# Attention on one core: where VectorE's copy of the next step's third transposes stands against the jump of its loop

## The chip, the cores and the metric

One Trainium2 chip, of which the kernel uses one core. The time is device microseconds from launch to end. Three runs of the kernel before gave a median of 2756.42 us (2753.38 to 2757.85).

## The reference, cut to what matters

128 graphs of 128 nodes with 512 features each go through attention with 16 heads of 32 (the adjacency added twice as a bias), a residual and a layer norm, then through one of four expert layers picked for each graph, batch norm statistics per expert, and a second residual and layer norm. All in float32.

```python
a = einsum('bhnd,bhmd->bhnm', q, k) * scale + (adj + adj)
p = softmax(a); o = einsum('bhnm,bhmd->bhnd', p, v)
x = layernorm(x + o @ Wo.T)
out = adj @ (x @ expert_w[top1(x)])
x = layernorm(x + relu(batchnorm_of_expert(out)))
```

The change touches the attention; the other stages are the same code in both kernels.

## The kernel before, in words

The kernel has three stages one after the other: `attention_phase` (L45), `expert_phase` (L636) and `norm_phase` (L907). Each engine has its own program, written out by hand, and engines meet only at semaphores.

In the attention a step is one graph. `for_steps` (L142) runs a loop of 15 rounds with 8 steps written out in each (`TAIL = 2 * UNROLL`), and then the last 8 steps written out behind the loop, without one. At the end of each round every engine jumps back to the start of its own loop.

What one step t does, as far as the change goes:

- TensorE transposes the softmax's 16 heads in four groups c = 0 to 3 into four PSUM banks (L292, semaphore `pt_ps`). With part of the values of step t+2 in between (L233), it multiplies the transposed groups with the values (`weighted_values`, L300), also in four groups. Group c waits at L297 until its transposes have been copied to SBUF: ScalarE copies the odd groups (L415, `pt_odd`), VectorE the even ones (L522, `pt_even`). Then come the scores of step t+1 (L244), the rest of the values, three passes of a projection of queries or keys (L225), the output projection (L356), which waits for `o_lo_done`, and three passes of a second projection.
- ScalarE, once the weighted values are there, writes their high part `o_hi` (L418).
- VectorE subtracts it to get the low part `o_lo` (L540), takes the minima of the 16 heads of step t+1 (L466), their largest values and the scales (L475 to L490), adds the residual (L566), takes the layer norm's statistics (L569 to L574), copies group 0 of the next step's transposes (L577, done at L522), evicts a projection (L580, done at L457) and writes the normalised graph `x1` (L584). In the kernel before, the copy of group 2 of the step's transposes stands at the head of the body (L529, done at L522), so in the first of the 8 steps it is the first thing after the jump. In the third step of every four, two casts of 128x1024 (L452) stand between this copy and L540.

So one line, L522, does both copies of a step, and it does group 2 directly behind L584 in the order of the program, with the jump between the two once in eight steps.

`build` (L1219) allocates SBUF in the order of the code. `adj_t` (L1227) is the expert stage's tile of transposed adjacencies; it is four slots of 136 float32 in each partition, 2176 bytes, and the first of all.

Of the kernel before, what the change touches and what calls it, by code (L numbers as in the profile page):

```python
# [18 lines left out]
F32 = mybir.dt.float32  # L19
# [6 lines left out]
P = 128  # L26
# [3 lines left out]
UNROLL = 4  # L30
# [14 lines left out]
def attention_phase(nc, io, W_hi, W_lo, w_stage, expert_w_in, ident, ones, g_x1, adj_t, hand_over, kept, pair,  # L45
# [11 lines left out]
    def columns(half):  # L57
        return slice(0, GN) if half is None else slice(half * HALF_N, (half + 1) * HALF_N)
# [21 lines left out]
    with ExitStack() as ctx:  # L80
# [69 lines left out]
        def exists(step, last, ahead):  # L150
            return not last or step + ahead < B

        def place_of(t, k, last):

            return (units_so_far(t) + k) % 2 if last else k % 2
# [283 lines left out]
        def _(dve):  # L439
# [5 lines left out]
            def rest_of_expert(e):  # L445
                dve.wait_ge(e_hi_done, e + 1)
                nc.vector.tensor_tensor(W_lo[:, e], w_stage[:, e % 2], W_hi[:, e].bitcast(F32),
                                        ALU.subtract).then_inc(e_lo_done, 1)

            def cut_xt(par, half):  # L450
                at = columns(half)
                nc.vector.tensor_copy(xt_hi[:, par, :, at], xt_stage[:, :, at]).then_inc(xt_hi_done, 1)  # L452

            def copy_qk(n, u, half, par):
                c, which, at = u % C, u // C, columns(half)
                dve.wait_ge(qk_ps, n + 1)
                nc.vector.tensor_scalar(qk[par][which][:, c, at], bank[BANK_A][:, at],  # L457
                                        HALF_SCALE if which == Q else 1.0, None, ALU.mult).then_inc(qk_done[1], 1)

            def minima(t, s):  # L460

                dve.wait_ge(adj_in[s], (t - s) * 4 + 16)
                dve.sem_inc(minima_begun, 1)
                for h in range(HEADS):
                    c, r = h // HC, h % HC
                    nc.vector.tensor_tensor_reduce(neg_s[:, h * P:(h + 1) * P],  # L466
                                                   bank[r][:, c * P:(c + 1) * P], adj_nat[:, s],
                                                   -2.0, BIG, ALU.add, ALU.min,
                                                   neg_max[:, h:h + 1]).then_inc(min_done, 1)
# [9 lines left out]
            def inverse(t, c):  # L479

                heads = slice(c * HC, (c + 1) * HC)
                dve.wait_ge(exp_done, HEADS * t + HC * (c + 1))
                nc.vector.reciprocal(inv_sum[:, heads], row_sum[:, heads]).then_inc(inv_done, 1)
# [36 lines left out]
            def copy_pt(t, c):  # L520
                dve.wait_ge(pt_ps, 4 * t + c + 1)
                nc.vector.tensor_copy(probs_t[:, c * D:(c + 1) * D], bank[c][:, :]).then_inc(pt_even, 1)  # L522

            copy_pt(0, 0)
            copy_qk(4 * C + 1, 1, None, 1)

            def body(t, s, i, g, last):
                more = exists(t, last, 1)
                copy_pt(t, 2)  # L529
                if s == 2 and not last:  # L530

                    dve.wait_ge(v_ps, t + 2)
                    dve.sem_inc(xt_turn, 1)
                    dve.wait_ge(xt_in, i * 16 + 32)
                    for half in range(2):
                        cut_xt(g, half)
                if last and t >= B - 2:
                    rest_of_expert(t - (B - 2))
                dve.wait_ge(o_hi_done, t + 1)
                nc.vector.tensor_tensor(o_lo[:, :, :], bank[BANK_O][:, :].rearrange("p (c n) -> p c n", c=C),  # L540
                                        o_hi[:, :, :].bitcast(F32), ALU.subtract).then_inc(o_lo_done, 1)
                if more:

                    dve.wait_ge(s_ps, t + 2)
                    minima(t + 1, (s + 1) % UNROLL)
                    largest(t + 1, 0)
                    inverse(t + 1, 0)
                    scales(t + 1, 0)
                    largest(t + 1, 1)
                    inverse(t + 1, 1)  # L550
                    scales(t + 1, 1)
                    largest(t + 1, 2)
                here = [(unit, k) for k, unit in enumerate(units_of_step(t, s, g, last)) if place_of(t, k, last) == 1]
                for unit, k in here:
                    if k == 0:
                        copy_qk(*unit)
                if more:
                    inverse(t + 1, 2)
                    scales(t + 1, 2)
                    largest(t + 1, 3)  # L560
                    inverse(t + 1, 3)
                    scales(t + 1, 3)

                dve.wait_ge(wo_ps, t + 1)
                dve.wait_ge(x_in[s], i * 16 + 16)
                nc.vector.tensor_tensor(res[:, s % 2], bank[BANK_WO][:, :], x_nat[:, s],  # L566
                                        ALU.add).then_inc(res_done, 1)
                dve.wait_ge(res_done, t + 2)
                nc.vector.bn_stats(stats[:, s % 2], res[:, s % 2]).then_inc(stats_done, 1)  # L569
                dve.wait_ge(stats_done, t + 1)  # L570
                dve.sem_inc(stats_go, 1)
                nc.vector.bn_aggr(mean_var[:, s % 2], stats[:, s % 2]).then_inc(mv_done, 1)
                dve.wait_ge(mv_done, t + 1)
                nc.vector.tensor_scalar(var_eps[:, s % 2:s % 2 + 1], mean_var[:, s % 2, 1:2], EPS, None,  # L574
                                        ALU.add).then_inc(ve_done, 1)
                if more:
                    copy_pt(t + 1, 0)  # L577
                for unit, k in here:
                    if k > 0:
                        copy_qk(*unit)  # L580

                dve.wait_ge(rstd_done, t + 1)
                dve.wait_ge(x1_out[s], i * 16 + 16)
                nc.vector.tensor_scalar(x1[:, s], res[:, s % 2], mean_var[:, s % 2, 0:1],  # L584
                                        rstd[:, s % 2:s % 2 + 1], ALU.subtract,
                                        ALU.mult).then_inc(x1_done, 1)

            for_steps(dve, body)
            rest_of_expert(V)
# [629 lines left out]
def build(nc, io, out_dram, B, D, E):  # L1219
    C = D // P  # L1220
    x1_dram = nc.dram_tensor("x1_scratch", [B, P, D], F32, kind="Internal").ap()
    y_dram = nc.dram_tensor("y_scratch", [B, P, D], F32, kind="Internal").ap()
    with ExitStack() as ctx:
        def sb(name, shape, dt=F32):
            return ctx.enter_context(nc.sbuf_tensor(name, shape, dt))

        adj_t = sb("adj_t", [P, UNROLL, P + 8])  # L1227
        w_stage = sb("w_stage", [P, 2, C, D])
        expert_w_in = [ctx.enter_context(nc.semaphore(f"expert_w_in{e}")) for e in range(E)]
        ident = sb("ident", [P, P])  # L1230
        ones = sb("ones", [P, P])
        expert_row = sb("expert_row", [1, B], U32)

        def sem(name):
            return ctx.enter_context(nc.semaphore(name))

        e_hi_done, e_lo_done = sem("e_hi_done"), sem("e_lo_done")
        g_x1_in = [sem(f"g_x1_in{i}") for i in range(UNROLL)]
        g_adj_in = [sem(f"g_adj_in{i}") for i in range(UNROLL)]
        ones_done = sem("ones_done")  # L1240
        hand_over = e_hi_done, e_lo_done, g_x1_in, g_adj_in, ones_done

        kept = sb("kept", [P, B // KEPT_EVERY, D])
        out_sum, out_sq = sb("out_sum", [P, E, D]), sb("out_sq", [P, E, D])
        with ExitStack() as cut:
            W_hi = cut.enter_context(nc.sbuf_tensor("w_hi", [P, 4, C, D], F32R))
            W_lo = cut.enter_context(nc.sbuf_tensor("w_lo", [P, 4, C, D], F32R))
            g_x1 = cut.enter_context(nc.sbuf_tensor("g_x1", [P, UNROLL, D], F32))
            attention_phase(nc, io, W_hi, W_lo, w_stage, expert_w_in, ident, ones, g_x1, adj_t, hand_over, kept, (out_sum, out_sq),
                            x1_dram, B, D)  # L1250
            expert_phase(nc, io, W_hi, W_lo, w_stage, expert_w_in, ones, expert_row, kept, out_sum, out_sq,
                         g_x1, adj_t, hand_over, x1_dram, y_dram, B, D, E)
        norm_phase(nc, io, ident, ones, expert_row, kept, out_sum, out_sq, x1_dram, y_dram, out_dram, B, D, E)
# [39 lines left out]
```

## Time and profile before

| | |
|---|---|
| median of 3 runs | 2756.42 us (2753.38 to 2757.85) |
| the profiled execution | 2755.41 us |
| its span, first to last instruction | 2753.7 us (1.7 us lie around it) |
| attention, experts, norm | to about 1990 us, to about 2500 us, to the end |
| TensorE, weight loads | busy 96% and 77% of the span |
| VectorE, ScalarE, GpSimd | busy 72%, 54%, 47% |
| granted TensorE clock, mean | 0.993 of full speed |

Busy time is a mean over three stages with different limits; each stage has to be read by itself. In a row of the timeline the first number is the start in us, the second the time from the start of the first to the end of the last instruction merged into it, "xN" how many are merged, and the bracket how long the engine had been idle and what ended that. "issue" means that the engine waited for nothing that the profile shows.

### The profile page before, as it was taken

The page shows a single profiled execution, that of the slowest core. Times are in us where ns is not written, and L with a number is a line of the kernel's source. Part 1 is how long each engine was busy: PE and PEld are TensorE (multiplying, and loading weights), DVE is VectorE, ACT ScalarE, POOL GpSimd, SP SyncE. Part 2 cuts the span into 40 slices and gives each one's busy share as a digit, 9 for nine tenths or more (in the row PEclk, how much of TensorE's full clock was granted, in tenths as well). Part 3 has the DMA queues.
Part 4 walks back from the last instruction along what each step waited for, and adds up shares of the span by engine and source line. Part 5 has one row for each costly group of instructions (what it writes and reads, how often), then busy time and mean ns, then how long its engine had stood idle before and what let it go on. Part 6 is the DMA issues. An engine that isn't in the chain of part 4 may idle for free. (4 is left out here: it accounts for less than half of the span.)

```text
span 2753.7 us, 71041 instructions
## 1 busy us (share of the span) xinstructions
PE 2642.7 (96%) x19802; PEld 2120.2 (77%) x19803; DVE 1994.9 (72%) x8230; ACT 1491.4 (54%) x5270; POOL 1298.3 (47%) x1174
## 2 busy tenths in 40 slices
PE   8999999999999999999999999999899999998776
PEld 7888888888888888888888888887688888884322
DVE  5888787888888888888887878888733333335887
ACT  4656565656556555656565656566544444442444
POOL 2344333334443434344333334443266666666887
PEclk9999999999999999999999999999999999999999
DMA  3111112111111121111112111112244444445999
GB/s 131 56 59 52 61 51 68 60 60 52 60 54 58 56 72 55 57 60 52 60 52 69 58 61 51 61 55 71 79 126 140 131 135 131 139 136 202 398 406 352
DMA packets 166057, 281.21 MB, mean 102 GB/s; under 512 B 18882, under 2 KB 52674, under 8 KB 161218
## 3 DMA queue, kind: packets, MB, share of 16 engines
q1 hardware_dynamic: 147266, 243.36, 26.4%
q10 hardware_dynamic: 18432, 33.56, 3.2%
q8 instruction: 164, 2.69, 0.4%
q14 instruction: 195, 1.60, 0.2%
HBM read 184.57 MB, written 92.27 MB: 101 GB/s over the span
## 5 line engine op out<-in xcount | busy, mean ns | idle before, releaser
L613 POOL TENSOR_TENSOR kept<-kept 128x512 f32<-128x512 f32 x512 | 532.8, 1041 | 1001.2 <-DVE kept L490 975.7
L380 ACT ACTIVATE kept<-kept 128x128 f32<-128x128 f32 x2048 | 793.2, 392 | 137.3 <-DVE kept L466 137.3
L466 DVE CUSTOM_DVE_ANT_0 kept<-att_bank,kept 128x128 f32<-128x128 f32 x2048 | 442.7, 286 | 1.8 <-PE att_bank L244 0.4
L380 ACT ACTIVATION_READ_ACCUMULATOR kept<-kept 128x1 f32 x2048 | 390.3, 191 | 0.0
L415 ACT ACTIVATE kept<-att_bank 128x512 f32<-128x512 f32 x256 | 153.1, 598 | 392.0 <-PE att_bank L292 392.0
L475 DVE TENSOR_REDUCE kept<-kept 128x4 f32<-128x512 f32 x512 | 347.2, 678 | 0.0
L225 PE MATMUL att_bank<-xt_hi,w_hi 128*128 128x512 f32 (+1 forms) x1080 | 280.0, 381 | 13.0 <-DVE w_lo L442 13.0
L225 PE MATMUL att_bank<-xt_lo,w_hi 128*128 128x512 f32 (+1 forms) x1080 | 277.8, 379 | 0.0
L225 PE MATMUL att_bank<-xt_hi,w_lo 128*128 128x512 f32 (+1 forms) x1080 | 277.6, 379 | 0.0
L292 PE MATMUL att_bank<-ident,kept 128*128 128x128 f32 x2048 | 246.0, 273 | 5.0 <-DVE kept L566 4.4
L292 PEld LDWEIGHTS att_bank<-ident,kept 128*128 128x128 f32 x2048 | 230.2, 140 | 25.0 <-DVE kept L566 5.6
L225 PEld LDWEIGHTS att_bank<-xt_hi,w_hi 128*128 128x128 f32 x1080 | 198.5, 189 | 53.4 <-issue 12.6
L540 DVE TENSOR_TENSOR o_lo<-att_bank,o_hi 128x512 fp32r<-128x512 f32 x128 | 88.5, 691 | 208.3 <-ACT o_hi L418 208.3
L225 PEld LDWEIGHTS att_bank<-xt_lo,w_hi 128*128 128x128 f32 x1080 | 198.0, 189 | 39.1
L225 PEld LDWEIGHTS att_bank<-xt_hi,w_lo 128*128 128x128 f32 x1080 | 197.5, 189 | 37.7
L418 ACT ACTIVATE o_hi<-att_bank 128x512 fp32r<-128x512 f32 x128 | 76.6, 599 | 249.3 <-PE att_bank L300 249.3
L522 DVE COPY kept<-att_bank 128x512 f32<-128x512 f32 x256 | 175.8, 687 | 47.3 <-issue 24.5
L606 POOL TENSOR_TENSOR xt_lo<-kept,xt_hi 128x1024 fp32r<-128x1024 f32 x64 | 163.6, 2577 | 98.0 <-DVE xt_hi L452 98.0
L1054 PE MATMUL ps_z<-n_y,ident 128*128 128x512 f32 x256 | 152.1, 678 | 54.9 <-POOL n_y L1174 52.4
L898 POOL TENSOR_TENSOR out_sum<-out_sum,g_out 128x512 f32 x96 | 123.7, 1289 | 134.6 <-ACT g_out L815 134.6
L827 DVE TENSOR_TENSOR products<-ps_y,router_w 128x16 f32<-128x16 f32 x128 | 22.8, 178 | 220.5 <-PE ps_y L741 220.4
L1209 ACT ACTIVATE n_x<-n_x,n_nb,n_rstd 128x512 f32<-128x512 f32 x128 | 104.2, 814 | 131.5 <-POOL n_nb L1191 80.2
(147 smaller groups left out, 5324.3 us busy)
## 6 DMA issues: line engine op xcount, KB each, us to landing
kept<-in_x SPq DMA_DIRECT2D x128, 256.0 KB, 2.6
x_scratch<-kept SPq DMA_DIRECT2D x128, 256.0 KB, 2.0
g_x<-x_scratch SPq DMA_DIRECT2D x128, 256.0 KB, 2.7
n_x<-x_scratch SPq DMA_DIRECT2D x128, 256.0 KB, 7.0
out_x<-n_x ACTq DMA_DIRECT2D x128, 256.0 KB, 5.5
kept<-in_x_t SPq DMA_DIRECT2D x31, 1024.0 KB, 5.2
y_scratch<-g_out SPq DMA_DIRECT2D x96, 256.0 KB, 2.0
n_y<-y_scratch SPq DMA_DIRECT2D x96, 256.0 KB, 6.6
```

Source lines behind the costliest of these rows:

```text
L225: mm = pe.matmul(dst, w[:, which, k, c * P:(c + 1) * P], x[:, par, k, at], start=m == 0, stop=m == len(todo) - 1)
L292: mm = pe.transpose(bank[c][:, r * P:(r + 1) * P], probs[:, h * P:(h + 1) * P], ident[:, :])
L380: nc.scalar.activation(probs[:, h * P:(h + 1) * P], neg_s[:, h * P:(h + 1) * P], ACT.Exp, bias=neg_max[:, h:h + 1], scale=-1.0, accum_out= ...
L415: nc.scalar.activation(probs_t[:, c * D:(c + 1) * D], bank[c][:, :], ACT.Copy).then_inc(pt_odd, 1)
L466: nc.vector.tensor_tensor_reduce(neg_s[:, h * P:(h + 1) * P], bank[r][:, c * P:(c + 1) * P], adj_nat[:, s], -2.0, BIG, ALU.add, ALU.min, n ...
L475: nc.vector.tensor_reduce(abs_max[:, heads], neg_s[:, c * D:(c + 1) * D].rearrange("p (h m) -> p h m", h=HC), AX_X, ALU.max, apply_absolut ...
L522: nc.vector.tensor_copy(probs_t[:, c * D:(c + 1) * D], bank[c][:, :]).then_inc(pt_even, 1)
L606: nc.gpsimd.tensor_tensor(xt_lo[:, par, :, at], xt_stage[:, :, at], xt_hi[:, par, :, at].bitcast(F32), ALU.subtract).then_inc(xt_lo_done, 1)
L613: nc.gpsimd.tensor_tensor(part, part, by, ALU.mult).then_inc(probs_done, 1)
L898: nc.gpsimd.tensor_tensor(acc, acc, src, ALU.add).then_inc(sum_done, 1)
L1054: pe.matmul(dst, ident[:, :], y[:, s], start=True, stop=False)
L1209: nc.scalar.activation(x1[:, s], x1[:, s], ACT.Identity, bias=nb[:, u, k:k + 1], scale=rstd[:, u, k:k + 1]).then_inc(out_done, 1)
```

## The change

VectorE's copy of group 2 for step t+1 is issued at the end of step t's body instead of at the head of step t+1's body; the copy of step 0 is issued once ahead of the loop. And `adj_t` is allocated behind `out_sq`, in the part of SBUF that the norm stage takes over, instead of ahead of everything.

```diff
             copy_pt(0, 0)
             copy_qk(4 * C + 1, 1, None, 1)
+            copy_pt(0, 2)
 
             def body(t, s, i, g, last):
                 more = exists(t, last, 1)
-                copy_pt(t, 2)
                 if s == 2 and not last:
...
                                         rstd[:, s % 2:s % 2 + 1], ALU.subtract,
                                         ALU.mult).then_inc(x1_done, 1)
+                if more:
+                    copy_pt(t + 1, 2)
 
             for_steps(dve, body)
...
-        adj_t = sb("adj_t", [P, UNROLL, P + 8])
         w_stage = sb("w_stage", [P, 2, C, D])
...
         with ExitStack() as cut:
+            adj_t = cut.enter_context(nc.sbuf_tensor("adj_t", [P, UNROLL, P + 8], F32))
             W_hi = cut.enter_context(nc.sbuf_tensor("w_hi", [P, 4, C, D], F32R))
```

## Rows read from the trace of the kernel before

**Rows 1.** Busy time by stretch: undisturbed attention steps; 106 steps with 14 jumps

```profile
core 0: us, PE busy (x) PEld busy (x) DVE busy (x) ACT busy (x) POOL busy (x), PEclk, DMA share, GB/s
161.06:1772.07 1611.01, 1596.52 (x13576) 1315.85 (x13572) 1317.57 (x5671) 957.65 (x3922) 632.74 (x582) 1.00 0.18 59
921.67:1011.83 90.16, 90.16 (x776) 74.56 (x772) 75.08 (x323) 54.20 (x222) 38.52 (x34) 1.00 0.16 53
```

**Rows 2.** Line L522, the copies: count, idle time before them, who waited

```profile
L522 DVE COPY kept<-att_bank x256: 679/690/693, 51.5 to 1973.7; 128x512 f32<-128x512 f32 x128
  issue: 24.5, 14
```

**Rows 3.** TensorE's waits in the attention loop, 60 to 1800 us: total, times, longest

```profile
PE att_bank L300 <- DVE kept L522: 14.1, 14, 1.2
```

**Rows 4.** VectorE's timeline around the jump at 903 us

```profile
901.14 0.69 DVE L522 COPY kept<-att_bank 128x512 f32<-128x512 f32 x1 [0.22 <-PE att_bank L292]
901.75 0.68 DVE L457 TENSOR_SCALAR out_sum<-att_bank 128x512 f32<-128x512 f32 x1
902.35 0.54 DVE L584 TENSOR_SCALAR kept<-kept,mean_var,rstd 128x512 f32<-128x512 f32 x1
904.58 0.69 DVE L522 COPY kept<-att_bank 128x512 f32<-128x512 f32 x1 [1.69 <-issue]
906.66 0.69 DVE L540 TENSOR_TENSOR o_lo<-att_bank,o_hi 128x512 fp32r<-128x512 f32 x1 [1.40 <-ACT o_hi L418]
```

**Rows 5.** VectorE's timeline one step later, without a jump

```profile
918.52 0.54 DVE L584 TENSOR_SCALAR kept<-kept,mean_var,rstd 128x512 f32<-128x512 f32 x1
918.98 0.68 DVE L522 COPY kept<-att_bank 128x512 f32<-128x512 f32 x1
921.67 0.69 DVE L540 TENSOR_TENSOR o_lo<-att_bank,o_hi 128x512 fp32r<-128x512 f32 x1 [2.01 <-ACT o_hi L418]
```

**Rows 6.** TensorE's timeline over the same two steps

```profile
889.59 1.17 PE L244 MATMUL att_bank<-w_stage,g_x 32*128 32x128 f32 x32
...
903.74 0.64 PE L300 MATMUL att_bank<-kept 128*32 128x128 f32 x16
905.33 0.64 PE L300 MATMUL att_bank<-kept 128*32 128x128 f32 x16 [0.94 <-DVE kept L522]
905.90 1.17 PE L244 MATMUL att_bank<-w_stage,g_x 32*128 32x128 f32 x32
...
911.23 1.07 PE L356 MATMUL att_bank<-w_hi,o_hi 128*128 128x512 f32 x4
...
919.89 1.08 PE L300 MATMUL att_bank<-kept 128*32 128x128 f32 x32
```

**Rows 7.** ScalarE's timeline at the jump at 903 us

```profile
902.45 0.60 ACT L415 ACTIVATE kept<-att_bank 128x512 f32<-128x512 f32 x1 [0.28 <-PE att_bank L292]
906.04 0.60 ACT L418 ACTIVATE o_hi<-att_bank 128x512 fp32r<-128x512 f32 x1 [2.98 <-PE att_bank L300]
```

**Rows 8.** VectorE: the copy after the longest and the shortest of 14 jumps; the loop's exit

```profile
418.46 0.69 DVE L522 COPY kept<-att_bank 128x512 f32<-128x512 f32 x1 [1.97 <-issue]
...
1269.13 0.69 DVE L522 COPY kept<-att_bank 128x512 f32<-128x512 f32 x1 [1.47 <-issue]
...
1874.56 0.68 DVE L522 COPY kept<-att_bank 128x512 f32<-128x512 f32 x1
```

**Rows 9.** VectorE by line and shape: one eviction into four tiles

```profile
L457 DVE TENSOR_SCALAR out_sum<-att_bank 128x512 f32<-128x512 f32 x31 | 21.1, 680 | 0.0
L457 DVE TENSOR_SCALAR w_stage<-att_bank 128x512 f32<-128x512 f32 x30 | 20.4, 680 | 0.0
L457 DVE TENSOR_SCALAR g_x<-att_bank 128x512 f32<-128x512 f32 x30 | 20.4, 680 | 0.0
```

**Rows 10.** Busy time by stretch: the norm stage and the expert stage (columns as in rows 1)

```profile
2560.00:2740.00 180.00, 136.56 (x307) 53.99 (x306) 150.89 (x355) 82.94 (x102) 157.22 (x154) 0.96 1.05 404
2010.00:2400.00 390.00, 390.00 (x2107) 332.45 (x2106) 145.10 (x703) 164.00 (x301) 254.46 (x202) 1.00 0.44 135
```

## The prediction, on record before the changed kernel ran

> **What bounds the kernel now.** I read the stages first, by busy time in stretches. Between two jumps of the attention loop TensorE is busy for all of six steps, 90.16 of 90.16 us, so a step there takes 90.16 / 6 = 15.03 us, while VectorE is busy for 75.08 us, 12.5 us in a step [rows 1]. TensorE sets the pace, and VectorE has room. Over 106 steps with 14 jumps in them TensorE is not fully busy: 1596.52 of 1611.01 us [rows 1]. At 15.027 us the 106 steps would take 1592.8 us; they take 18.2 us more, 1.3 us for each jump.
>
> Next, who makes TensorE wait. In this loop there is one large wait: the weighted values wait 14 times, 14.1 us in all, for VectorE's copy of the transposes [rows 3]. Then, why that copy is late. Of the 256 copies 14 stand behind an idle time that no semaphore ended, 24.5 us together, 1.75 us each [rows 2]. The timeline shows which: group 2's copy in the first step of a round. L584 ends at 902.89 us and the copy starts at 904.58 us, after 1.69 us [rows 4]. In the step after, the same two instructions follow each other without a gap [rows 5], and so they do where the loop is left and nothing jumps [rows 8]. 15 rounds have 14 jumps back. What the copy reads was ready long before: ScalarE, which waits for group 3's transposes, later than group 2's, took them at 902.45 us [rows 7]. So the gap is VectorE's jump.
>
> Last, what the gap does to TensorE. Group 0's matmuls start at 903.74 us; the second half (groups 2 and 3), which needs the late copy, starts at 905.33 us, 1.59 us later. Without a jump all 32 follow each other [rows 6]: the row is 1.08 us long against 0.64 us for half of them, so the second half starts 0.44 us after the first. The late copy costs 1.59 - 0.44 = 1.15 us here.
>
> **The change, part by part.** *Removed:* the gap ahead of the copy in 14 steps. The order of VectorE's instructions, the semaphores and their counts stay as they are; the copy issues no DMA and passes no queue; SP's store of x1 waits for L584, which stands ahead of the copy in both kernels. Only the jump moves, behind the copy. With it there, the copy follows L584 as in rows 5, 0.46 us after its start: at about 902.81 us, done at 903.50 us. TensorE wants it at 903.74 + 0.44 = 904.18 us, so 0.68 us of room is left, and the stall goes.
>
> The size of the stall has two ends. The 14.1 us that TensorE's own waits give are the lower one [rows 3]: that view counts idle time after the modelled end of the matmuls before, so it leaves out part of the delay (0.94 us in the row where the starts show 1.15 us). The upper one is the 18.2 us by which the 14 rounds are too long [rows 1], if all of that is VectorE's doing. Not all is: in this round group 0 itself, which waits for no late copy, starts 14.15 us after the scores before it (889.59 to 903.74 us), against 13.99 us a step later (905.90 to 919.89 us) [rows 6]. These 0.16 us come before the stall and stay; 14 x 0.16 = 2.2 us. I take 18.2 - 2.2 = **16.0 us**; 14 x 1.15 = 16.1 us agrees.
>
> *Added:* the jump ahead of L540. What hides it: after the copy, L540 waits for ScalarE's `o_hi`, and that for TensorE, 2.01 us in a step without a jump [rows 5]. The 14 gaps lie between 1.47 and 1.97 us [rows 8], all below 2.01 us, and VectorE may reach the jump a little earlier, since the instruction ahead of it is then 0.69 us long and not 0.54 us [rows 4]. Cost 0. If the cover is short by some tenths, they fall into the next rooms: the output projection wants `o_lo` at 911.23 us, and L540 ends at 907.35 us [rows 4, 6]; the next copy has 0.65 us (it ends at 919.66 us, its matmuls start at 919.89 + 0.44 us [rows 5, 6]). L540 would have to be over 0.65 us late, a jump of over 2.66 us, before TensorE felt it. Behind the copy's own wait only the jump and L540 are queued, and its transposes are in time [rows 7].
>
> What a jump is made of the trace does not say. *The Trainium skill, "Runtime: NRT & Kernel Launch", section "Instruction fetch mechanics", says that a taken branch whose target is not among the two pages held makes the sequencer fetch the page first, a stall. It speaks against getting rid of the jump's price by moving it: by it the same stall stands ahead of L540. With the room of rows 5 it gives the same sum.*
>
> *Ahead of the loop* group 2's copy of step 0 is issued where it was executed anyway: 0. *The last 8 steps* have no jump and keep their order: 0.
>
> *`adj_t`:* the tiles from `w_stage` to `out_sq` and those of the norm stage start 2176 bytes lower in each partition, the others stay. For the engines I take 0: the same eviction takes 680 ns into three tiles at different places [rows 9]. For DMAs no row compares places; the attention's run at a share of 0.18 [rows 1] and the experts' at 0.44 beside a fully busy TensorE [rows 10], so only the norm stage (share 1.05, 404 GB/s [rows 10]) could feel it, either way. I take 0, the nearest thing measured, and put the other end among the rivals.
>
> *Sum:* 16.0 us off the profiled execution's 2755.4 us is 2739.4 us. The median of the runs shown lies 1.0 us above that execution, so like runs would have 2740.4 us; I say **2740 us**.
>
> **The rivals.** *A, the gap is not the jump's and goes with the copy* (something that the first step of a round does ahead of that copy alone). For it: "issue" names no cause. Against it: the gap is missing at the loop's exit, with the same code behind it [rows 8]. TensorE would wait as before: 2755 us. *By the Trainium skill, "Advanced Engine Details and Errata", section "Control Flow Timing", a compare-and-branch takes about 108 ns; with that as the whole jump the change would give 14 x 0.108 = 1.5 us, by an estimate from that page, and the time would be 2754 us. The gaps of 1.47 to 1.97 us do not agree with it as the whole price.* Chance 6%.
>
> *B, the jump is dearer in its new place*, because the loop's start now lies elsewhere in the code and its first instructions come in two loads instead of one. Two gaps are 2 x 1.75 = 3.50 us [rows 2]: L540 would be 3.50 - 2.01 = 1.49 us late, the next copy 1.49 - 0.65 = 0.84 us too late for TensorE. Of 1.15 us for each jump 0.31 us would be won, 14 x 0.31 = 4.3 us: 2751 us. For it: the gaps differ by 0.5 us with nothing in the code to say why. Against it: every one of the 14 is below the cover. 6%.
>
> *C, slower: the lower addresses slow the norm stage's DMAs.* That stage runs at the DMAs' limit for 180 us [rows 10]. To come out slower by over 5.5 us it has to lose 16.0 + 5.5 = 21.5 us, so its transfers would have to take over 12% longer; at 15% it would lose 27 us, and the time would be 2755.4 - 16.0 + 27.0 = 2766 us. For it: no row excludes it. Against it: nothing in the rows makes a place in SBUF matter [rows 9]. 3%.
>
> **How the numbers follow.** The forecast has 85%. Its own range: 14.1 to 18.2 us off 2755.4 us, 2737.2 to 2741.3 us, widened by the 2 us by which the runs differ and the 1.0 us to the median, 2735 to 2744 us. B lies above it at 2751 us, with shares of a second load in between, so I let the range reach to 2746 us: **2735 to 2746 us**. About 0.2%, 5.5 us, is what a measurement here can tell from no change. Faster by more: the forecast and a small part of B, 87%. Within: A and most of B, 10%. Slower: C, 3%.
>
> **What would show it.** Right: in the first step of a round the copy follows L584 without a gap; the idle time ahead of L540 in that step is about 2.0 us, as in other steps; TensorE's wait for L522 in the loop is gone; a round falls from 8 x 15.03 + 1.3 = 121.5 us to about 120.4 us. The steps fail one by one: if "issue" still stands ahead of L522, A; if L540 is ended by "issue" and starts over 0.65 us late, B; if the rounds are shorter and the norm stage longer, C. If rounds shrink by 1.3 us and not 1.15 us, the 0.16 us were VectorE's too, and the gain is the upper end.

## The result, and the profile after

| | before | after |
|---|---|---|
| median (lowest to highest) | 2756.19 us (2753.38 to 2757.85, 4 runs) | 2739.20 us (2738.39 to 2740.26, 4 runs) |
| ratio | | 0.994, 95% interval 0.9922 to 0.9957 |
| the profiled execution, its span | 2755.41 us, 2753.7 us | 2738.80 us, 2737.0 us |

The forecast was 2740 us, in a range of 2735 to 2746 us. The changed kernel is faster by 17.0 us, 0.6%.

The stretch of 106 steps that holds the 14 jumps, by busy time in stretches (columns as in [rows 1]: length, then PE, PEld, DVE, ACT, POOL):

```profile
159.57:1754.84 1595.27, 1594.20 (x13576) 1316.70 (x13572) 1313.26 (x5671) 957.81 (x3922) 632.93 (x582) 1.00 0.18 59
```

It answers to the 1611.01 us of [rows 1]: 15.74 us less, and TensorE is busy in all but 1.1 us of it. The line of the copies, and then TensorE's waits in the loop, 60 to 1800 us, both of the changed kernel:

```profile
L522 DVE COPY kept<-att_bank x256: 679/684/692, 50.0 to 1956.7; 128x512 f32<-128x512 f32 x128
its engine sat idle before it (us, times) until:
  PE att_bank L292: 14.1, 39
```

```profile
PE att_bank L292 <- issue: 0.9, 4, 0.3
```

The 24.5 us by "issue" ahead of L522 [rows 2] are gone, and so are the 14.1 us of TensorE's waits for it [rows 3]. (The 14.1 us in the line above are another wait: 39 short ones of VectorE for TensorE's transposes.) VectorE's timeline around a jump of the changed kernel:

```profile
893.64 0.54 DVE L584 TENSOR_SCALAR kept<-kept,mean_var,rstd 128x512 f32<-128x512 f32 x1
894.09 0.68 DVE L522 COPY kept<-att_bank 128x512 f32<-128x512 f32 x1
896.81 0.69 DVE L540 TENSOR_TENSOR o_lo<-att_bank,o_hi 128x512 fp32r<-128x512 f32 x1 [2.03 <-ACT o_hi L418]
```

This is a step with a jump, and it looks like the step without one in [rows 5]: the copy directly behind L584, then 2.03 us that ScalarE ends. The jump is inside those 2.03 us. One has to know that it is there to find it, since the view gives the whole idle time to what ended it.

The two spans differ by 16.6 us. The 106 steps give 15.74 us of it. 1.49 us were won ahead of them: the same L540 from which the stretch is counted starts at 159.57 us and not at 161.06 us. The rest of the program lost 0.6 us. Nothing ties the 1.49 us to the change: the first experiment found the early and the late start in both places of `adj_t`.

### The profile page after: what moved, and what is told of

Read it like the earlier page. It is cut to its first block and busy times, and to the rows that moved or that the text cites. A ratio compares the mean times of both kernels' runs of the same rounds, so it can differ in the third digit from the quotient of the medians.

```text
span 2737.0 us, 71026 instructions
## 1 busy us (share of the span) xinstructions
PE 2641.8 (97%) x19802; PEld 2120.9 (77%) x19803; DVE 1991.8 (73%) x8230; ACT 1491.7 (55%) x5270; POOL 1301.2 (48%) x1174
## 5 line engine op out<-in xcount | busy, mean ns | idle before, releaser
L292 PE MATMUL att_bank<-ident,kept 128*128 128x128 f32 x2048 | 246.0, 273 | 6.0 <-DVE kept L566 4.7
L292 PEld LDWEIGHTS att_bank<-ident,kept 128*128 128x128 f32 x2048 | 230.1, 140 | 26.6 <-DVE kept L566 5.9
L540 DVE TENSOR_TENSOR o_lo<-att_bank,o_hi 128x512 fp32r<-128x512 f32 x128 | 88.4, 691 | 218.3 <-ACT o_hi L418 218.3
L522 DVE COPY kept<-att_bank 128x512 f32<-128x512 f32 x256 | 175.7, 686 | 22.7 <-PE att_bank L292 14.1
```

The source lines that it names most:

```text
L292: mm = pe.transpose(bank[c][:, r * P:(r + 1) * P], probs[:, h * P:(h + 1) * P], ident[:, :])
```

## The experiments

Ratios are against the kernel before, run on the same chip.

**1. Each half of the change alone.** In `copy_only` the copy is moved and `adj_t` stays the first tile; in `place_only` only `adj_t` is moved.

```diff
 copy_only, against the changed kernel
+        adj_t = sb("adj_t", [P, UNROLL, P + 8])
         w_stage = sb("w_stage", [P, 2, C, D])
...
-            adj_t = cut.enter_context(nc.sbuf_tensor("adj_t", [P, UNROLL, P + 8], F32))
 place_only, against the kernel before: the same two lines the other way round
```

> The copy moved as in the change, adj_t left where it was. Theory (the whole gain is the jump taken off TensorE's path): as the changed kernel, 2739 us, 0.994 of before; in the attention loop TensorE's wait for L522 is gone, the 106 steps take about 1595.3 us as in the changed kernel. Rival (the lower addresses carry part of it, such as the 1.5 us by which the changed kernel's first weights were split earlier): 1.5 us or more above the changed kernel, with the steps equally long.

> Only adj_t moved, the copy at the head of the body as before. Theory: as before, 2756 us, ratio 1.000 within 0.001; 14 gaps of 1.75 us ahead of the copy and 14 us of waits of TensorE for it. Rival (addresses matter for the first loads or for the norm stage's DMAs): at least 1.5 us faster, with the first W_lo written about 1.5 us earlier, or a norm stage longer or shorter by some us.

Measured: `copy_only` 2738.3 us, ratio 0.9938 (0.9924 to 0.9951); `place_only` 2756.82 us, ratio 1.0003 (0.9994 to 1.0012). The 106 steps, first of `copy_only`, then of `place_only`:

```profile
159.44:1754.17 1594.73, 1593.94 (x13576) 1316.69 (x13572) 1313.24 (x5671) 957.62 (x3922) 632.67 (x582) 1.00 0.18 59
```

```profile
160.34:1772.10 1611.76, 1596.50 (x13576) 1315.78 (x13572) 1317.62 (x5670) 958.11 (x3922) 633.77 (x582) 1.00 0.18 59
```

The copy alone gives the whole gain and the tile's place gives none. What of the 1.5 us at the start? The first split of a weight, L442 on VectorE, in the kernel before and in the changed kernel:

```profile
10.58 2.29 DVE L442 TENSOR_TENSOR w_lo<-w_stage,w_hi 128x2048 fp32r<-128x2048 f32 x1 [5.55 <-ACT w_hi L369]
```

```profile
9.03 2.29 DVE L442 TENSOR_TENSOR w_lo<-w_stage,w_hi 128x2048 fp32r<-128x2048 f32 x1 [3.77 <-ACT w_hi L369]
```

`copy_only`, with the tile in its old place, has the early start as well (9.11 us), and two of the kernels below with the tile in its new place have the late one (10.56 us in `delay_16`, 10.52 us in `jump_behind_low`). So the start differs from execution to execution in both layouts, and no row ties it to the tile. What makes it differ stays open.

**2. Is the jump still paid?** `probe_1` puts one tiny copy behind the jump that waits for nothing, so that the time until it starts is the jump's own.

```diff
                 more = exists(t, last, 1)
+                if s == 0 and g == 0 and not last:
+                    nc.vector.tensor_copy(res[:, 0, 0:1], ident[:, 0:1])
```

> The changed kernel with one more instruction on VectorE at the head of every eighth step, a copy of one element per partition that waits for no semaphore, so that the gap ahead of it is the jump's own. Theory: the jump still costs VectorE its time: a gap by issue of 1.4 to 1.9 us ahead of that copy 14 times, nothing ahead of it in the first round; L540 still starts when the high part is there; time as the changed kernel, 2739 us within 2. Rival (behind the copy the jump is no longer dear): gaps under 0.5 us, same time.

Measured: 2740.29 us, one run. The probe's line:

```profile
L531 DVE COPY kept<-ident x15: 144/154/155, 52.7 to 1738.9; 128x1 f32<-128x1 f32 x15
its engine sat idle before it (us, times) until:
  issue: 21.8, 14
```

VectorE still loses 21.8 / 14 = 1.56 us at each jump and the time is that of the changed kernel: the price is paid, and nothing waits for it. It is 0.19 us less than ahead of the copy (1.75 us, [rows 2]).

The rows of VectorE's sequencer (DVEq), in which the loop's own instructions stand, say why the visible part depends on what stands ahead. L144 is the loop; these are VectorE's rows of it in the kernel before, 890 to 910 us (count, shortest/median/longest in ns, start of the first and of the last):

```profile
L144 DVEq COMPARE_BRANCH  x1: 63/63/63, 901.7 to 901.7; - x1
L144 DVEq FUSED_REGOPS  x1: 74/74/74, 904.5 to 904.5; - x1
```

The branch itself takes 63 ns, but the sequencer's next instruction comes 2.8 us after it, and the copy at 904.58 us. VectorE's sequencer got to the branch at 901.7 us, when L584 was queued and not yet begun [rows 4]. The queued work, until 902.89 us, covered 1.2 us; the 1.69 us by "issue" in [rows 4] are what was left. In between, instructions are fetched: a DMA queue of the kind "instruction" in the same kernel, 902.5 to 903.2 us (packets, MB, share of 16 engines):

```profile
q14 instruction: 1, 0.01, 3.9%
```

In the trace of that kernel one such packet of 8 KB starts 0.99 to 1.01 us behind each of the 14 branches, and the next instruction follows 2.77 to 2.97 us behind the branch. The packet itself takes 0.32 to 0.55 us; what fills the rest of the 2.8 us no row shows.

The Trainium skill has two pages on this. "Advanced Engine Details and Errata", section "Control Flow Timing", gives about 108 ns for a compare-and-branch; the branch's own row agrees with that order, the jump as a whole does not. "Runtime: NRT & Kernel Launch", section "Instruction fetch mechanics", says that a branch to a page not held has to wait for its fetch; the trace agrees, with one fetch seen about 1 us behind the branch and 2.8 us in all.

**3. How much cover is there?** The cover is VectorE's wait ahead of L540, behind which the jump hides; the room is how late L540 may come beyond it before TensorE waits. `delay_16` puts a reduction of 2.29 us behind the jump, ahead of L540, in every eighth step.

```diff
+                if s == 0 and g == 0 and not last:
+                    nc.vector.tensor_reduce(res[:, 0, 0:HEADS], ident[:, :].unsqueeze(1).to_broadcast([P, HEADS, P]),
+                                            AX_X, ALU.max)
```

> The changed kernel with a reduction of 16 x 128 elements (about 2.2 us, by the 0.68 us of L475 for 512) at the head of every eighth step on VectorE, behind the jump and ahead of L540. Theory (cover of 2.0 us ahead of L540, then room of 0.65 us at the next copy): jump 1.6 us and 2.2 us are 3.8 us, so L540 is 1.8 us late, the next copy 1.15 us too late for TensorE, which waits for L522 14 or 15 times in the step after the jump: 16 us more than the changed kernel, about 2755 us. Rival (VectorE has 2.5 us free in each step and swallows it): under 3 us more, no wait of TensorE for L522.

Measured: 2753.0 us, 13.8 us more than the changed kernel. TensorE's waits, 60 to 1800 us:

```profile
PE att_bank L292 <- DVE kept L569: 12.0, 14, 0.9
```

The size was nearly right, the place was not. L540 is late by 1.56 + 2.29 - 2.03 = 1.82 us, and 13.8 / 14 = 0.99 us of it reach TensorE, so the room is 0.83 us. But TensorE does not wait for L522. It waits at the head of the next step, at its transposes, for the residual (L569 here, L566 in the kernel before), since L311 asks for `res_done` ahead of everything else. That wait comes before the copies' one and takes up the whole delay.

**4. The jump where nothing hides it.** `jump_behind_low` moves L540 in front of the jump too.

```diff
                 if more:
                     copy_pt(t + 1, 2)
+                    low(t + 1, s == 1, i, g, last)
```

Here `low` holds the casts of the third step and L540, which are taken out of the head of the body, and is called once ahead of the loop.

> The changed kernel with L540 (the low part of the weighted values) and the casts ahead of it moved in front of the jump too, so that the jump stands between L540 and the minima. Theory (the jump keeps its price of about 1.7 us and the wait for ScalarE's high part is what hides it in the changed kernel): here nothing hides it; a gap by issue of about 1.7 us ahead of the first of the minima, 14 times; the next copy is 1.7 - 0.65 = 1.05 us too late for TensorE, 14 x 1.05 = 15 us more than the changed kernel, about 2754 us. Rival (the price belonged to the copy standing first behind the jump, or any later place hides it): no gap, 2739 us.

Measured: 2804.43 us, ratio 1.0177 (1.0162 to 1.0193), 65 us more than the changed kernel and not 15. The order is the only difference, and in the seven steps of eight without a jump it is the same order. VectorE's and TensorE's waits, 60 to 1830 us:

```profile
DVE kept L466 <- issue: 64.3, 14, 5.2
```

```profile
PE att_bank L356 <- ACT kept L386: 37.5, 14, 3.3
PE att_bank L292 <- DVE kept L569: 3.5, 4, 0.9
```

The rival, that any later place hides the jump, falls. But the gap is 4.6 us each and not 1.7 us, and TensorE's waits of 41 us explain less than 65 us. The first has two parts. With L540 in front, VectorE's sequencer stands at L540's wait for ScalarE and gets to the branch only when L540 starts (176.37 us, the branch 176.5 us), so that nothing but L540 itself, 0.69 us, covers the 2.8 us. And the jump itself was longer, in the same rows of L144:

```profile
L144 DVEq COMPARE_BRANCH  x1: 62/62/62, 176.5 to 176.5; - x1
L144 DVEq FUSED_REGOPS  x1: 63/63/63, 181.3 to 181.3; - x1
```

Unrounded, from 176.46 us to 181.33 us, these are 4.9 us. At that time a load of 1 MB was on the DMA engines. SyncE's issues of that load, here and then in the changed kernel, where VectorE's branch is at 171.5 us:

```profile
174.82 0.34 SPq L166 DMA_DIRECT2D kept<-in_x_t  x1
```

```profile
173.37 0.34 SPq L166 DMA_DIRECT2D kept<-in_x_t  x1
```

Here the branch (176.46 us) comes 1.6 us behind the load's issue; in the changed kernel it comes 1.9 us ahead of it. The DMA queues of `jump_behind_low` from 176.4 to 179.0 us, and then from 179.0 to 179.7 us:

```profile
q1 hardware_dynamic: 116, 0.94, 90.4%
```

```profile
q8 instruction: 1, 0.02, 10.5%
q14 instruction: 2, 0.02, 5.6%
```

For 2.6 us after the branch only data moved, at 90% of the engines; then the instructions came. The rest of the 65 us lies behind TensorE's wait at L356. From the first matmul of L356 to the next transposes it took 7.21 us in that step (183.82 to 191.03 us), against 5.44 us in the changed kernel (901.38 to 906.82 us): 1.77 us more. A part of that is TensorE's clock: the granted clock of a stretch of 6.2 us behind the wait is 0.72, so a part of it ran at 1.2 instead of 2.4 GHz:

```profile
183.80:190.00 6.20, 6.17 (x20) 4.93 (x21) 5.68 (x27) 5.46 (x27) 3.38 (x4) 0.72 0.00 0
```

The 14 steps are not all alike. In ten the granted clock behind the wait is down, to 0.62 at the lowest (first row); in four it stays at 1.00 (second row):

```profile
683.00:692.00 9.00, 7.83 (x22) 6.21 (x23) 8.18 (x40) 6.60 (x32) 4.16 (x5) 0.62 0.04 3
1184.00:1192.00 8.00, 5.76 (x24) 4.43 (x24) 7.49 (x43) 7.16 (x34) 3.48 (x4) 1.00 0.00 0
```

Those four are the steps in which TensorE then waits for the residual (3.5 us in all), and they too take 6.63 us from L356 to the transposes, 1.19 us more than in the changed kernel. Over all 14 that stretch takes 7.26 us in the mean, 1.82 us more. So 1.19 us of it would have come at the full clock too, and by this estimate 14 x 0.63 = 9 us of the 65 are the clock's. Counted by starts, L356 itself is 2.87 us late in the mean, and the sum is 14 x (2.87 + 1.82) = 66 us.

**5. Was it the load?** `low_xt_later` is the same kernel with the load issued one step later; `xt_later` is the changed kernel with that edit alone.

```diff
-                if s == 0 and not last:
+                if s == 1 and not last:
                     sp.wait_ge(xt_lo_done, i * 2 + 4)
                     load_xt(i + 2)
```

> The kernel with the jump behind L540 again, with SyncE's load of 1 MB of transposed inputs (L192) issued in the second step of every four instead of the first. Theory (the gaps of 4.6 us there are a jump of 2.8 us whose code waits behind this load, which was on the DMA engines from 1.9 us before the jump to 3 us after it): the gaps ahead of the minima fall to 2.2 to 2.5 us, TensorE waits under 1 us at L356 and keeps its full clock, and 14 x 1.7 us remain over the changed kernel: about 2763 us, 2755 to 2768. Rival (a jump is dearer when VectorE has nothing queued as it reaches it): gaps of 4.6 us, 2804 us as before.

> The control: the changed kernel with the same move of SyncE's load. Theory: VectorE's jump is over before that load starts in the changed kernel, so nothing changes, 2739 us within 2. Rival (the load's place matters by itself): another time by over 2 us.

Measured: `low_xt_later` 2771.63 us, ratio 1.0063 (1.0046 to 1.008); `xt_later` 2739.89 us, ratio 0.9947 (0.993 to 0.9964). Waits of VectorE and of TensorE in `low_xt_later`, 60 to 1830 us:

```profile
DVE kept L466 <- issue: 38.9, 14, 3.0
```

```profile
PE att_bank L292 <- DVE kept L569: 12.5, 14, 0.9
PE att_bank L356 <- ACT kept L386: 12.2, 14, 1.1
```

The gaps fell from 4.6 to 2.78 us, TensorE kept its clock over the loop (1.00, shown at the end), and 33 us of the 65 went away; the control did not move. So the load's place made the jump longer. The rest was mis-sized: 2.2 to 2.5 us of gap and 1.7 us of cost were expected, 2.78 and 2.3 us came (32.4 / 14), which is 9 us more than expected and above the range given. The expectation counted the jump alone; in this kernel it took 3.0 us (175.0 to 178.0 us by L144's rows), and two more instructions of the sequencer (L462, L463) stand between it and the minima. And TensorE waits twice, 12.2 / 14 = 0.87 us for the values at L356 and 12.5 / 14 = 0.89 us for the residual at L292. This view counts only from the modelled end of the matmuls; by their starts L356 is 1.07 us late in the mean and the stretch behind it takes 6.63 us instead of 5.44 us, 2.26 us together.

**6. Fewer jumps.** The loop of one engine alone is written out for 24 steps, so that it has 4 jumps back instead of 14: VectorE's in the kernel before (`dve_24`), TensorE's in the changed kernel (`pe_24`, the same edit with `nc.tensor`).

```diff
-            with eng.Fori(0, LAST // TAIL) as i:
-                for s in range(TAIL):
-                    body(i * TAIL + s, s % UNROLL, i * 2 + s // UNROLL, s // UNROLL, False)
+            n = 3 * TAIL if eng is nc.vector else TAIL
+            with eng.Fori(0, LAST // n) as i:
+                for s in range(n):
+                    body(i * n + s, s % UNROLL, i * (n // UNROLL) + s // UNROLL, s // UNROLL % 2, False)
```

> The kernel before, with VectorE's loop alone written out for 24 steps instead of 8: 5 rounds, 4 jumps back instead of 14; the copy still stands first behind each. Theory (each jump costs TensorE 1.15 us there): 10 x 1.15 = 11.5 us less than before, about 2745 us, 4 gaps ahead of L522 and 4 waits of TensorE. Rival (the gap belongs to the first of eight steps, not to the jump): as before, 14 gaps, 2756 us.

> The changed kernel with TensorE's loop alone written out for 24 steps: 4 jumps back instead of 14. Theory (the 2.4 us that the changed loop still takes over 106 x 15.027 us is TensorE's own jump, up to 0.5 us in some rounds): about 1.7 us less than the changed kernel, 2737.5 us, late first transposes in at most 4 steps. Rival (the late transposes come from what they wait for, GpSimd's scaling or VectorE's residual): nothing won, 2739 us, still 8 or 9 late steps.

Measured: `dve_24` 2743.2 us, ratio 0.9961 (0.9946 to 0.9976); `pe_24` 2738.36 us, ratio 0.9938 (0.9925 to 0.9952). VectorE's waits and the 106 steps in `dve_24` (the copy's line is L523 there), then the 106 steps of `pe_24`:

```profile
DVE kept L523 <- issue: 7.1, 4, 2.2
```

```profile
158.80:1758.40 1599.60, 1594.99 (x13576) 1316.42 (x13572) 1316.35 (x5670) 958.00 (x3922) 633.73 (x582) 1.00 0.18 59
```

```profile
159.47:1752.41 1592.94, 1592.85 (x13576) 1317.09 (x13572) 1313.57 (x5670) 957.84 (x3922) 632.90 (x582) 1.00 0.18 59
```

Ten jumps fewer took ten gaps and 11.4 us of the 106 steps away (1611.01 to 1599.60 us): the gap belongs to the jump, and rival A, which had lost its "issue" ahead of L522 in the changed kernel, falls a second time. In `pe_24` the 106 steps take 1592.94 us, against 1592.83 us for 106 x 15.027, so the 2.4 us that the changed loop still had are put down to TensorE's own jumps. Two things weaken this: four jumps are left in `pe_24`, and yet nearly all of the 2.4 us went; and with all 14 of them the excess was 1.9 us in `copy_only` and 1.0 us in `xt_later` (1593.84 us), so it differs between executions. The whole kernel's time shows it too weakly to count: 2738.36 against 2739.20 us, with intervals that overlap. No version was found that is clearly faster than the changed kernel.

## Why the prediction was right

- *What bounds the kernel:* right. With the wait gone, TensorE is busy for 1594.20 of 1595.27 us.
- *The gap is VectorE's jump:* right. It is gone from L522, it stands in front of whatever is first behind the jump (`probe_1`), and it goes with the number of jumps (`dve_24`).
- *The size, 16.0 us:* the 106 steps became 15.74 us shorter, and 16.28 us shorter in `copy_only`. The upper end, 18.2 us, would have needed that the whole excess was VectorE's. The 2.2 us set aside for what is late before the copy, read off one step, measured 2.4 us here and 1.0 to 1.9 us in other executions; `pe_24` points to TensorE's jump, while the prediction had left them without a cause. The lower end, 14.1 us, was too low for the reason given, the matmuls' modelled ends.
- *Nothing at the jump's new place:* right. The gap there is 1.56 us against a cover of 2.03 us. The slight shortening that was expected, 0.15 us, came as 0.19 us. But the prediction took the visible gap for the jump's price. That the trace does not say what a jump is made of was not so: the rows of L144 and the packet of instructions (experiment 2) are in the trace of the kernel before, and they put the price at 2.8 us, with 1.2 us of it behind queued work. The forecast did not suffer, since work was queued ahead of the jump in its new place too; the expectation of `jump_behind_low` did.
- *The rooms behind the cover:* the size was about right, the place was wrong. The prediction expected 0.65 us at the next copy (its own rows give 919.89 + 0.44 - 919.66 = 0.67 us) and overlooked that TensorE waits for the residual at the head of each step; `delay_16` ran into that wait first, with a room of 0.83 us. Nothing in the forecast hung on it, since the cover sufficed.
- *`adj_t` at nothing:* right (`place_only`, 1.0003). In the changed kernel 180 us of the norm stage (from 2543 us) show 400 GB/s against 404 GB/s in [rows 10]. From TensorE's first matmul of that stage to the end it takes 257.0 us, 1.2 us more than before (255.8 us), but 257.5 us in `copy_only` too, where the tile is in its old place. Rival C, which needed 21.5 us, falls.
- *Rival B, a dearer jump,* did not come true, but a dearer jump was nearer than it said, for another reason: not by where the code lies, but with a load of 1 MB under way, the price rose from 2.8 to 4.9 us in `jump_behind_low`.

A part of the agreement in the whole time is luck. Of the 16.6 us between the two profiled executions 15.74 us are the steps, 1.49 us an early start that differs between executions, and 0.6 us were lost elsewhere; the forecast held neither of the last two, and they partly cancel. What bears out the prediction are the steps and the experiments, not the 0.8 us between 2740 and 2739.2 us.

## What to carry to other kernels

A loop's jump cost VectorE about 3 us here, of which the work queued ahead of it hid a part, so its place matters: put it where the engine will wait for another one anyway, behind the last thing that the bottleneck engine needs from this engine and ahead of an instruction that has a long wait. The sign of a jump is idle time by "issue" in the first step of each round; the gain is not that idle time (24.5 us here) but the amount by which the round with the jump is longer on the bottleneck engine, less what that engine's own jump takes. And before moving an instruction over a jump, look at which transfers start at that time: the jump takes a fetch of instructions, and here it stood behind a load.

## What the runs showed of the hardware that was not expected

A jump on VectorE takes 2.8 us from the branch to the next instruction (2.77 to 2.97 us in the 14 rounds of the kernel before), and 4.9 us behind a load of 1 MB (4.1 to 5.5 us in the 14 rounds of `jump_behind_low`); moving the load by one step took the gap from 4.6 to 2.78 us. TensorE's branch shows its own price in its row: 3.6 us in the median of 15 rounds (kernel before, the loop's line), of which 0.07 to 0.17 us for each jump show in the 106 steps (1.0 to 2.4 us in 14, experiment 6).

```profile
L144 PEldq COMPARE_BRANCH  x15: 83/3569/4010, 167.1 to 1868.3; - x15
```

And a wait of TensorE can cost more than its length. In `jump_behind_low` the granted clock was down behind ten of the 14 waits at L356, and the stretch to the next transposes took 6.97 to 8.46 us there, against 6.63 us behind the other four. The length of the wait alone does not tell the two apart: behind 2.76 us (309.12 us) the clock stayed at 1.00, behind 2.00 us (433.19 us) it fell, to 0.79 over the next 8 us. In `delay_16` and `low_xt_later`, with waits of at most 0.9 and 1.1 us, it did not fall in the loop, and in `low_xt_later` the granted clock of the loop's 1624.60 us was 1.00:

```profile
161.40:1786.00 1624.60, 1599.08 (x13543) 1312.46 (x13545) 1312.64 (x5661) 956.58 (x3919) 632.68 (x582) 1.00 0.18 57
```
